# Attention layers of a twelve-layer stack: row maxima by half a batch, normalisation a batch ahead, one clamp a head, and another order of work in a head pair's step

## The chip, the cores and the metric

The kernel runs on one core of one Trainium2 chip and does the whole stack in one launch. The metric is device time in microseconds (us). Three runs of the kernel before took 2915.75, 2919.40 and 2923.68 us, with a median of 2919.4 us. The engines are TensorE (PE, with its weight loads as PEld), VectorE (DVE), ScalarE (ACT), GpSimd (POOL) and SyncE (SP), which issues most DMAs. Each engine takes its instructions in program order, and waits at the head of its queue until the semaphores that an instruction names have been counted up.

## The reference, cut to what matters

The input x is 8 batches of 256 tokens by 128 features. Twelve layers are added to it one after the other. Five of them are touched:

```python
def _L0_xattn_ref / _L3_xattn_ref(x, ctx, ...):      # 16 heads of 8, 512 context rows per batch
    q = x @ Wq + bq; k = ctx @ Wk + bk; v = ctx @ Wv + bv          # heads split after
    attn = softmax(q @ k.T * scale, axis=-1)                        # 256 x 512 per head
    out = (attn @ v) @ Wo + bo
def _L1_attn_ref(x, Wk, Wq, Wo, bo):                  # 16 heads of 8 over the 256 tokens, v = k
def _L2_attn_ref(x, Wq, Wkv, Wo, bo):                 # 16 heads of 64, causal, 256 x 256 per head
def _L3_attn_ref(x, w_down_q, w_down_kv, w_up_q, ...):# 16 heads of 64, low rank, rotary, not causal
    x = x + layer(layernorm(x))                       # for each; L2_attn: out / (sum + 1e-8)
```

In `L0_xattn` the probabilities are also held above a floor, exp(bounded max - clamp), that differs from row to row and head to head; this is the `clamp` branch of the kernel. The other seven layers (a gated recurrence, two single-head attentions, four feed-forward layers) are not touched.

## The kernel before

The layers run one after the other, each in its own block, with x (8 x 256 x 128) staying in SBUF. Within a layer every engine's program is a loop over steps n from FIRST to LAST, so the order on each engine is written out by hand. What one engine owes another is counted in semaphores. Two functions hold all five layers.

**16 heads of 8: `layer_attention_heads8` (L615 on), used by L0_xattn, L1_attn and L3_xattn.** One step is one head, so 128 steps carry the exponentials. Queries and keys are projected once per batch, split into three bf16 parts each (ACT L1123, L1125, then `split` at L813, L814, L816), written to DRAM in another order (`stage`, L754 and L760) and read back to all partitions (`spread`, L769 and L773). This preparation of a batch is the jobs T (transpose of the normalised rows), Q, K and V, all through the one PSUM bank `psM`. Each head is scored twice. The first time, LEAD steps ahead, PE L1045 puts queries on partitions and DVE L920 (L922 in L1_attn) takes the row maximum. When all 16 heads of a batch have their maxima, the job M turns them (PE L1027), they are negated and split into three bf16 parts (DVE L937 or ACT L1114, then POOL L851 to L857), and SP writes them as three more rows of the queries (`max_rows`, L780). The second time PE L1057 makes the turned scores with the maximum already subtracted, ACT L1160 takes the exponential, and PE L1071 (`weigh`) multiplies two heads with V. LEAD is H + 6 = 22 steps in the two layers with context and H + 10 = 26 in L1_attn; so 22 (26) steps pass with maxima alone before the first exponential, and as many at the end without maxima. In L0_xattn ACT makes the floor (L1146), SP writes it to DRAM and spreads all 16 heads' floors, 2 MB, over the partitions (L784, L787), and DVE L931 clamps each half head (128 x 512). In L3_xattn the result takes a way over DRAM (ACT L1140 out, SP L796 back, jobs A and O). `norm` on POOL normalises a batch at its own job T, and all copies of V are filled with ones by POOL (L866) before the first batch's splits. PE and DVE wait for all weights (`NLOAD`) before their first work.

**16 heads of 64: `layer_attention_heads64` (L174 on), used by L2_attn (causal) and L3_attn.** One step is one pair of heads, 64 steps in all, 8 in a batch. PE's step n: scores of pair n (L501), the jobs of slot n, `weigh` of pair n-2 (L536), the spread of 1/sum of pair n-2 over partitions (`spread_inverse`, L542), in the causal layer the blocking of later keys (L511), and the turning of pair n-1's probabilities (L521). Jobs are P (a later pair's projections, L468 or L475, in every step), V (values, L484, in steps 2 and 7 of a batch in L3_attn and in steps 0, 2, 3 and 7 in L2_attn), T and C (transpose, down-projection for the next batch), and O (output, L487, in steps 3 and 5); they share two PSUM banks `psA`. The product and the spread inverse lie in one bank, `psOR`. ACT copies the product out (`copy_out`, L601) after its exponentials (L588), and DVE multiplies that copy with the spread inverse (`combine`, L415) as the first thing of the next step, before it copies the turned probabilities (L400, causal) and takes the maxima (L392). In L3_attn DVE reads P into `rotc` and `rots` (L380), POOL adds them to `qk` (`rotate`, L306) and then widens the inverse (`widen`, L311).

## Time and profile before

The profiled execution took 2914.34 us, and the span of its trace is 2912.6 us. The five layers that are touched take 1876 us of it:

| layer | from, us | to, us | length, us | PE busy, us | DVE busy, us | POOL busy, us | granted TensorE clock |
|---|---|---|---|---|---|---|---|
| L0_xattn | 138.7 | 571.9 | 433.2 | 336.7 | 363.1 | 97.4 | 0.87 |
| L1_attn | 902.4 | 1123.9 | 221.5 | 186.2 | 116.1 | 62.5 | 0.85 |
| L2_attn | 1390.1 | 1784.2 | 394.1 | 346.8 | 219.5 | 52.3 | 0.98 |
| L3_attn | 2011.7 | 2447.9 | 436.2 | 356.3 | 239.9 | 149.2 | 0.93 |
| L3_xattn | 2448.8 | 2840.2 | 391.4 | 330.7 | 195.5 | 73.0 | 0.86 |

A layer begins when the one before has ended, so a layer's length is the sum of its steps, and what one step gains or loses comes back as often as it is repeated. Busy time of PE includes the pipeline's depth and is an upper bound of its work. The clock is a share of 2.4 GHz, and TensorE has two levels, 1.2 and 2.4 GHz: 0.87 means that it ran at the lower one for a part of the stretch.

### The profile page before, as it was taken

The numbers are of one execution on the slowest core, as the hardware profiler recorded it, in microseconds if no ns is written. First come the engines' busy times: TensorE is split into PE (matmuls) and PEld (weight loads), VectorE is DVE, ScalarE is ACT, GpSimd is POOL, SyncE is SP. The second block draws the span as 40 slices with busy tenths as digits, with TensorE's granted clock in tenths as the row PEclk, the third lists the DMA queues.
The fourth block names the chain that finished last, engine by engine and source line by source line (L and its number), as shares of the span: only waits on it lengthen the run. The fifth ranks groups of instructions, "written<-read, shape, count | busy, mean of one in ns | idle before, by whom it ended". The sixth has DMA issues, their size and how long they took to land. (4 is left out here: it accounts for less than half of the span.)

```text
span 2912.6 us, 40706 instructions
## 1 busy us (share of the span) xinstructions
PE 2224.6 (76%) x13779; PEld 1382.4 (47%) x13779; DVE 1690.1 (58%) x3810; ACT 1174.3 (40%) x2898; POOL 522.7 (18%) x703
## 2 busy tenths in 40 slices
PE   4668888789996897534799994936888886898982
PEld 2424343367774454423566663625555654344441
DVE  5568999633434562877456556562665554754524
ACT  3114444445552564211344441410555553354550
POOL 1122220000002410121111101011333322212100
PEclk9759999899997898866899997965999998698995
DMA  0043323110002310000000001011000001332200
GB/s 27 12 116 86 115 77 92 50 40 1 1 1 62 76 46 28 8 0 0 31 1 1 1 1 28 1 27 34 1 1 1 1 1 38 85 75 63 53 11 17
DMA packets 109272, 95.63 MB, mean 33 GB/s; under 512 B 61414, under 2 KB 96526, under 8 KB 105742
## 3 DMA queue, kind: packets, MB, share of 16 engines
q1 hardware_dynamic: 75790, 91.99, 12.2%
q10 hardware_dynamic: 33280, 1.05, 0.5%
q8 instruction: 113, 1.85, 0.3%
q14 instruction: 89, 0.73, 0.1%
HBM read 77.21 MB, written 14.81 MB: 32 GB/s over the span
## 5 line engine op out<-in xcount | busy, mean ns | idle before, releaser
L920 DVE TENSOR_REDUCE L_xattn_mx<-L_xattn_psS 128x1 f32<-128x512 f32 x512 | 326.9, 684 | 152.9 <-PE L_xattn_psS L1045 148.7
L1160 ACT ACTIVATE L_xattn_PT<-L_xattn_psT 128x512 f32<-128x512 f32 x512 | 284.7, 598 | 170.8 <-PE L_xattn_psT L1057 163.6
L1071 PE MATMUL L_xattn_psO<-L_xattn_PT,L_xattn_V 128*32 128x256 f32 x2048 | 264.1, 404 | 40.8 <-DVE L_xattn_PT L931 40.8
L588 ACT ACTIVATE L_attn_pr<-L_attn_psS,L_attn_negm 128x256 f32<-128x256 f32 (+1 forms) x512 | 222.4, 447 | 175.4 <-PE L_attn_psS L511 92.0
L1045 PE MATMUL L_xattn_psS<-L_xattn_KR,L_xattn_QR 72*128 72x512 bf16 x512 | 224.0, 441 | 56.3 <-DVE L_xattn_mx L920 30.0
L1057 PE MATMUL L_xattn_psT<-L_xattn_QR,L_xattn_KR 75*128 75x256 bf16 x1024 | 198.7, 283 | 3.0 <-ACT L_xattn_PT L1160 2.0
L1875 DVE TENSOR_TENSOR L_ffn_wt<-L_ffn_act,L_ffn_cw 128x512 f32<-128x512 f32 x128 | 88.5, 692 | 183.8 <-ACT L_ffn_act L1992 172.4
L1071 PEld LDWEIGHTS L_xattn_psO<-L_xattn_PT,L_xattn_V 128*32 128x32 f32 x2048 | 118.4, 115 | 154.6 <-issue 61.2
L931 DVE SCALAR_TENSOR_TENSOR L_xattn_PT<-L_xattn_PT,L_xattn_floor_w 128x512 f32<-128x512 f32 x256 | 178.4, 741 | 16.1 <-DMA L_xattn_floor_w<-L_xattn_staged_floor 11.6
L392 DVE TENSOR_REDUCE L_attn_mx<-L_attn_psS 128x2 f32<-128x512 f32 x256 | 164.4, 684 | 40.0 <-PE L_attn_psS L501 40.0
L415 DVE TENSOR_TENSOR L_attn_aoT<-L_attn_raw,L_attn_psOR 128x256 f32<-128x256 f32 x128 | 54.0, 422 | 222.7 <-ACT L_attn_raw L601 222.7
L501 PE MATMUL L_attn_psS<-L_attn_qk 64*128 64x256 f32 x1024 | 147.4, 405 | 30.0 <-ACT L_attn_pr L588 30.0
L1950 PE MATMUL L_ffn_psY<-L_ffn_wdn,L_ffn_fT 128*128 128x128 f32 x1024 | 138.4, 279 | 15.5 <-ACT L_ffn_fT L1997 8.6
L536 PE MATMUL L_attn_psOR<-L_attn_prT,L_attn_V 128*64 128x256 f32 (+1 forms) x1024 | 139.1, 382 | 7.3 <-DVE L_attn_prT L400 4.9
L1057 PEld LDWEIGHTS L_xattn_psT<-L_xattn_QR,L_xattn_KR 75*128 75x128 bf16 x1024 | 101.0, 102 | 80.1 <-issue 20.2
L1992 ACT ACTIVATE L_ffn_act<-L_ffn_psU 128x512 f32<-128x512 f32 x128 | 76.5, 597 | 145.6 <-PE L_ffn_psU L1925 145.6
L1045 PEld LDWEIGHTS L_xattn_psS<-L_xattn_KR,L_xattn_QR 72*128 72x128 bf16 x512 | 52.1, 102 | 173.2 <-DVE L_xattn_mx L920 111.8
L1950 PEld LDWEIGHTS L_ffn_psY<-L_ffn_wdn,L_ffn_fT 128*128 128x128 f32 x1024 | 125.1, 193 | 19.1 <-ACT L_ffn_fT L1997 10.3
L1925 PE MATMUL L_ffn_psU<-L_ffn_wup,L_ffn_hT 128*128 128x512 f32 x256 | 132.7, 602 | 0.0
L306 POOL TENSOR_TENSOR L_attn_qk<-L_attn_rotc,L_attn_rots 128x512 f32<-128x512 f32 x64 | 81.3, 1270 | 237.4 <-PE L_attn_psOR L542 130.3
L501 PEld LDWEIGHTS L_attn_psS<-L_attn_qk 64*128 64x128 f32 x1024 | 94.3, 188 | 58.5 <-issue 54.6
L521 PE MATMUL L_attn_psT<-ident,L_attn_pr 128*128 128x128 f32 x896 | 120.9, 276 | 0.0
(537 smaller groups left out, 4342.8 us busy)
## 6 DMA issues: line engine op xcount, KB each, us to landing
L_xattn_KR<-L_xattn_k_parts SPq DMA_DIRECT2D x96, 192.0 KB
L_xattn_floor_w<-L_xattn_staged_floor SPq DMA_DIRECT2D x8, 2048.0 KB, 8.2
L_xattn_QR<-L_xattn_q_parts SPq DMA_DIRECT2D x32, 288.0 KB
L_xattn_k_parts<-L_xattn_ks SPq DMA_DIRECT2D x48, 128.0 KB, 2.6
L_xattn_ctxT<-in_ctx SPq DMA_DIRECT2D x24, 192.0 KB, 2.4
L_attn_QR<-L_attn_q_parts SPq DMA_DIRECT2D x16, 288.0 KB
L_attn_KR<-L_attn_k_parts SPq DMA_DIRECT2D x48, 96.0 KB
L_xattn_q_parts<-L_xattn_qs SPq DMA_DIRECT2D x48, 64.0 KB, 2.5
```

Source lines behind the costliest of these rows:

```text
L392: link.mark(nc.vector.reduce_max(mx[:, n % 4, :, r], psS[g % 3][:], AX.X))
L501: ins = nc.tensor.matmul(psS[g % 3][:, t], qk[b % 2][at, j, 0, t * P:(t + 1) * P], qk[b % 2][at, j, 1], start=(t == 0 or not causal), stop ...
L536: ins = nc.tensor.matmul(psOR[r * DH:(r + 1) * DH, 0, first:S], V[b % 2][:, k, hd * DH:(hd + 1) * DH], prT[n % 2][:, r, k * S:k * S + widt ...
L588: ins = nc.scalar.activation(pr[n % 3][:, r, t, 0:width], psS[(2 * n + r) % 3][:, t, 0:width], ACT.Exp, bias=negm[:, n % 4, t, r:r + 1], s ...
L920: nc.vector.reduce_max(mx[:, b % 2, u, hd:hd + 1], psS[n % 2][:], AX.X).then_inc(s_used, 1)
L931: nc.vector.scalar_tensor_tensor(at, at, 1.0, floor_w[b % 2][:, hd, None, :].to_broadcast((P, 2, S)), ALU.min, ALU.max).then_inc(clamped, 1)
L1045: ins = nc.tensor.matmul(psS[n % 2][:, i * keys:(i + 1) * keys], QR[b % NB][0:PAIR, hd, t * P:(t + 1) * P], KR[b % NB][0:PAIR, hd, :], sta ...
L1057: ins = nc.tensor.matmul(psT[n % NPS][:, k], KR[b % NB][0:ROWS, hd, kt * P:(kt + 1) * P], QR[b % NB][0:ROWS, hd, :], start=True, stop=True)
L1071: ins = nc.tensor.matmul(psO[r:r + HW, g % 2], V[b % NV][:, kt, n % H], PT[(n * NU + kt // 2) % NPT][:, kt % 2], start=(kt == 0), stop=(kt ...
L1160: nc.scalar.activation(PT[i % NPT][:], psT[i % NPS][:], ACT.Exp).then_inc(exp_ready, 1)
L1925: nc.tensor.matmul(psU[n % 2][:], hT[b % 2][:, t * P:(t + 1) * P], wup[:, g * EG:(g + 1) * EG].rearrange("p e f -> p (e f)"), start=True, ...
L1950: ins = nc.tensor.matmul(psY[tile % 2][:, 0:D], fT[n % 3][:, k], wdn[:, g * BK + k], start=False, stop=(g == NGR - 1 and k == BK - 1))
```

## The change

**16 heads of 64.** A slot's jobs are parted into `early` (P) and `late` (all others; before step 0 all are early). PE's step is now: scores of n, spread inverse of n-2, early jobs, `weigh` of n-2, the blocking, late jobs, turning of n-1. ACT copies the spread inverse instead of the product (`copy_spread`), ahead of its jobs and exponentials; `weigh` waits for that copy, and `spread_inverse` waits for the `combine` of the pair before. DVE multiplies the product, read from PSUM, with the copy, for pair n-2 in step n, behind maxima, early jobs and the inverse.

**16 heads of 8.** LEAD falls by 8 steps, to HH + 6 = 14 and HH + 10 = 18 (HH = 8). The job M, the split of the maxima, their rows and the floors go by halves of a batch, 16 of each instead of 8. PREP goes from 42 to 38 and from 60 to 52 steps ahead. With context a batch is prepared in the order K, T, Q, and its K and Q DMAs change places. The floor's spread is 1 MB. A clamp takes a whole head (128 x 1024), and the probability tiles hold a head. Loads are waited for in three groups (`qk_loaded`, `v_loaded`, `o_loaded`), keys' and queries' first. POOL fills the first V ahead of the second `norm`, the others behind the first batch's splits, and normalises batch b+1 at the job Q of batch b.

```diff
@@ layer_attention_heads64
+    for n in range(0, LAST):
+        slots[n].sort(key=lambda group: group[0][0] != "P")
+    early = {n: [group for group in slots[n] if n < 0 or group[0][0] == "P"] for n in slots}
+    late = {n: [group for group in slots[n] if n >= 0 and group[0][0] != "P"] for n in slots}
...
             def combine(n):
                 b, j = n // NP, n % NP
-                dve.wait_ge(raw_ready, n + 1)
-                dve.wait_ge(r_ready, n + 1)
+                dve.wait_ge(pv_done, n + 1)
                 if j == 0 and b >= 2:
                     await_job(dve, ("O", b - 2, TB - 1))
-                nc.vector.tensor_tensor(aoT[b % 2][:, j], raw[n % 2][:], psOR[:, 1], ALU.mult).then_inc(ao_ready, 1)
+                nc.vector.tensor_tensor(aoT[b % 2][:, j], psOR[:, 0], spread[n % 2][:], ALU.mult).then_inc(ao_ready, 1)
...
             for n in range(FIRST, LAST):
-                if 0 <= n - 3 < NN:
-                    combine(n - 3)
                 if causal and 0 <= n - 2 < NN:
                     copy_turned(n - 2)
                 if 0 <= n < NN:
                     maxima(n)
-                for group in slots[n]:
+                for group in early[n]:
                     for job in group:
                         read(job)
                 if 0 <= n - 1 < NN:
                     invert(n - 1)
+                if 0 <= n - 2 < NN:
+                    combine(n - 2)
+                for group in late[n]:
+                    for job in group:
+                        read(job)
...
-                wait(pe, ao_ready, n)
+                pe.wait_ge(spread_ready, n + 1)
...
             def spread_inverse(n):
                 pe.wait_ge(rinv_ready, n + 1)
+                wait(pe, ao_ready, n)
...
                 if 0 <= n < NN:
                     scores(n)
-                for group in slots[n]:
+                if 0 <= n - 2 < NN:
+                    spread_inverse(n - 2)
+                for group in early[n]:
                     run(group)
                 if 0 <= n - 2 < NN:
                     weigh(n - 2)
-                    spread_inverse(n - 2)
                 if causal and 0 <= n < NN:
                     block_later(n)
+                for group in late[n]:
+                    run(group)
...
-            def copy_out(n):
+            def copy_spread(n):
                 act.wait_ge(r_ready, n + 1)
                 wait(act, ao_ready, n - 1)
-                nc.scalar.copy(raw[n % 2][:], psOR[:, 0]).then_inc(raw_ready, 1)
+                nc.scalar.copy(spread[n % 2][:], psOR[:, 1]).then_inc(spread_ready, 1)
@@ layer_attention_heads8
-    NPS, NPT = 3, 10 if NU == 2 else 8
+    NPS, NPT = 3, 5 if NU == 2 else 8
-    LEAD, PREP, STAGE, DVE_SPLITS = (H + 6, 42, 3, 2) if from_ctx else (H + 10, 60, 6, 3)
+    LEAD, PREP, STAGE, DVE_SPLITS = (HH + 6, 38, 3, 2) if from_ctx else (HH + 10, 52, 6, 3)
...
-        for i, kind in enumerate("TQK"):
+        for i, kind in enumerate("KTQ" if from_ctx else "TQK"):
             jobs[at + i * (b > 0)].append((kind, b, 0))
...
-        jobs[H * b - LEAD + H + 1].append(("M", b, 0))
+        for i in range(2):
+            jobs[H * b + HH * i - LEAD + HH + 1].append(("M", b, i))
...
-        stage_at = at + 2 + STAGE if b else FIRST
+        stage_at = min(at + 2 + STAGE, prep_step(b + 1) + 1) if b else FIRST
...
-        moves[H * b - LEAD + H + 1].append(("rows", b, 0))
+        for i in range(2):
+            moves[H * b + HH * i - LEAD + HH + 1].append(("rows", b, i))
...
                 for i in range(PARTS):
-                    sp.dma_start(QR[b % NB][PAIR + i:PAIR + i + 1], mp[:, i]).then_inc(m_rows, 16)
+                    sp.dma_start(QR[b % NB][PAIR + i:PAIR + i + 1, hf * HH:(hf + 1) * HH], mp[:, i]).then_inc(m_rows[hf], 16)
                 if clamp:
...
-                    wait(sp, clamped, NU * H * (b - 1))
-                    sp.dma_start(floor_w[b % 2][:].rearrange("p h s -> p (h s)"),
-                                 rows(f_dram.rearrange("h s -> (h s)")).to_broadcast((P, H * S))).then_inc(floor_spread, 16)
+                    wait(sp, clamped, HH * (n - 1))
+                    sp.dma_start(floor_w[n % 2][:].rearrange("p h s -> p (h s)"),
+                                 rows(f_dram.rearrange("h s -> (h s)")).to_broadcast((P, HH * S))).then_inc(floor_spread, 16)
...
             norm(0)
+            nc.gpsimd.memset(V[0][:], 1.0).then_inc(v_set, 1)
             norm(1)
-            for i in range(NV):
+            pool.wait_ge(k_split, SPLITS)
+            pool.wait_ge(q_split, SPLITS)
+            for i in range(1, NV):
                 nc.gpsimd.memset(V[i][:], 1.0).then_inc(v_set, 1)
...
-                    if kind == "T" and b >= 2:
-                        norm(b)
...
+                    if kind == "Q" and 1 <= b < B - 1:
+                        norm(b + 1)
...
-                nc.vector.scalar_tensor_tensor(at, at, 1.0, floor_w[b % 2][:, hd, None, :].to_broadcast((P, 2, S)), ALU.min, ALU.max).then_inc(clamped, 1)
+                nc.vector.scalar_tensor_tensor(at, at, 1.0, floor_w[half % 2][:, n % HH, None, :].to_broadcast((P, NKT, S)), ALU.min, ALU.max).then_inc(clamped, 1)
...
-            pe.wait_ge(loaded, 16 * NLOAD)
...
+                if b == 0 and kind in "QK":
+                    pe.wait_ge(qk_loaded, 16 * WQK)
```

The order of PE in one step of L3_attn with a value job, before: scores, P (wq, wk), values, `weigh`, spread inverse, turning.

```order
L501 MATMUL L_attn_psS<-L_attn_qk 128x256 x4
L475 MATMUL L_attn_psA<-L_attn_cT,L_attn_wq 128x256 x2
L475 MATMUL L_attn_psA<-L_attn_cT,L_attn_wk 128x256 x2
L484 MATMUL L_attn_psA<-L_attn_wv,L_attn_cT 128x512 x2
L536 MATMUL L_attn_psOR<-L_attn_prT,L_attn_V 64x256 x4
L542 MATMUL L_attn_psOR<-ident,L_attn_rinv 128x128 x2
L521 MATMUL L_attn_psT<-ident,L_attn_pr 128x128 x8
```

The same step on PE in the changed kernel, whose line numbers are a few higher (L507 scores, L549 spread inverse, L481 P, L542 `weigh`, L490 values, L527 turning):

```order
L507 MATMUL L_attn_psS<-L_attn_qk 128x256 x4
L549 MATMUL L_attn_psOR<-ident,L_attn_rinv 128x128 x2
L481 MATMUL L_attn_psA<-L_attn_cT,L_attn_wq 128x256 x2
L481 MATMUL L_attn_psA<-L_attn_cT,L_attn_wk 128x256 x2
L542 MATMUL L_attn_psOR<-L_attn_prT,L_attn_V 64x256 x4
L490 MATMUL L_attn_psA<-L_attn_wv,L_attn_cT 128x512 x2
L527 MATMUL L_attn_psT<-ident,L_attn_pr 128x128 x8
```

The spread inverse has moved from behind `weigh` to right behind the scores, and the values from ahead of `weigh` to behind it.

PE in L2_attn, before, in the step that has an output and a value job (L487, L484), up to the scores of the next step:

```order
L501 MATMUL L_attn_psS<-L_attn_qk 128x256 x4
L487 MATMUL L_attn_psA<-L_attn_wo,L_attn_aoT 128x128 x8
L468 MATMUL L_attn_psA<-L_attn_hT,L_attn_wq 128x256
L468 MATMUL L_attn_psA<-L_attn_hT,L_attn_wk 128x256
L484 MATMUL L_attn_psA<-L_attn_wv,L_attn_hT 128x512
L536 MATMUL L_attn_psOR<-L_attn_prT,L_attn_V 64x256 x2
L536 MATMUL L_attn_psOR<-L_attn_prT,L_attn_V 64x128 x2
L542 MATMUL L_attn_psOR<-ident,L_attn_rinv 128x128 x2
L511 MATMUL L_attn_psS<-L_attn_maskb,identb 128x128 x4
L521 MATMUL L_attn_psT<-ident,L_attn_pr 128x128 x6
```

The same step in the changed kernel:

```order
L507 MATMUL L_attn_psS<-L_attn_qk 128x256 x4
L549 MATMUL L_attn_psOR<-ident,L_attn_rinv 128x128 x2
L474 MATMUL L_attn_psA<-L_attn_hT,L_attn_wq 128x256
L474 MATMUL L_attn_psA<-L_attn_hT,L_attn_wk 128x256
L542 MATMUL L_attn_psOR<-L_attn_prT,L_attn_V 64x256 x2
L542 MATMUL L_attn_psOR<-L_attn_prT,L_attn_V 64x128 x2
L517 MATMUL L_attn_psS<-L_attn_maskb,identb 128x128 x4
L493 MATMUL L_attn_psA<-L_attn_wo,L_attn_aoT 128x128 x8
L490 MATMUL L_attn_psA<-L_attn_wv,L_attn_hT 128x512
L527 MATMUL L_attn_psT<-ident,L_attn_pr 128x128 x6
```

The blocking of later keys (maskb), for which the exponentials wait, now stands ahead of the output and value jobs instead of behind them.

PE ahead of the first turned scores of L0_xattn, before (L1045 scores for maxima, two a head; L1018 K, L1030 T, L1016 Q, L1021 V, L1027 the job M of all 16 heads, L1057 the first turned scores):

```order
L1018 MATMUL L_xattn_psM<-L_xattn_ctxT,L_xattn_wk 128x512
L1045 MATMUL L_xattn_psS<-L_xattn_KR,L_xattn_QR 128x512 x18
L1030 MATMUL L_xattn_psM<-ident,L_xattn_h 128x128 x2
L1045 MATMUL L_xattn_psS<-L_xattn_KR,L_xattn_QR 128x512 x2
L1016 MATMUL L_xattn_psM<-L_xattn_hT,L_xattn_wq 128x256
L1045 MATMUL L_xattn_psS<-L_xattn_KR,L_xattn_QR 128x512 x2
L1018 MATMUL L_xattn_psM<-L_xattn_ctxT,L_xattn_wk 128x512
L1045 MATMUL L_xattn_psS<-L_xattn_KR,L_xattn_QR 128x512 x4
L1021 MATMUL L_xattn_psM<-L_xattn_wv,L_xattn_ctxT 128x128 x4
L1045 MATMUL L_xattn_psS<-L_xattn_KR,L_xattn_QR 128x512 x2
L1027 MATMUL L_xattn_psM<-ident,L_xattn_mx 16x128 x2
L1045 MATMUL L_xattn_psS<-L_xattn_KR,L_xattn_QR 128x512 x11
```

The same stretch in the changed kernel (L1092 scores, L1068 V, L1065 K, L1077 T, L1063 Q, L1074 the job M of 8 heads, L1104 the first turned scores):

```order
L1063 MATMUL L_xattn_psM<-L_xattn_hT,L_xattn_wq 128x256
L1092 MATMUL L_xattn_psS<-L_xattn_KR,L_xattn_QR 128x512 x10
L1068 MATMUL L_xattn_psM<-L_xattn_wv,L_xattn_ctxT 128x128 x4
L1065 MATMUL L_xattn_psM<-L_xattn_ctxT,L_xattn_wk 128x512
L1092 MATMUL L_xattn_psS<-L_xattn_KR,L_xattn_QR 128x512 x2
L1077 MATMUL L_xattn_psM<-ident,L_xattn_h 128x128 x2
L1074 MATMUL L_xattn_psM<-ident,L_xattn_mx 8x128 x2
L1092 MATMUL L_xattn_psS<-L_xattn_KR,L_xattn_QR 128x512 x2
L1063 MATMUL L_xattn_psM<-L_xattn_hT,L_xattn_wq 128x256
L1092 MATMUL L_xattn_psS<-L_xattn_KR,L_xattn_QR 128x512 x9
L1104 MATMUL L_xattn_psT<-L_xattn_QR,L_xattn_KR 128x256 x2
```

M now follows 8 heads' scores instead of 16, and V stands next to K, T next to M, which before stood steps apart.

## Rows read from the trace of the kernel before

**Rows 1.** Windows of four layers: us, each engine's busy time, PE clock, DMA share, GB/s.
```profile
138.70:571.90 433.20, 336.69 (x2032) 159.92 (x2032) 363.14 (x637) 180.61 (x345) 97.38 (x122) 0.87 0.31 89
...
1390.10:1784.20 394.10, 346.76 (x2384) 241.38 (x2384) 219.51 (x592) 168.26 (x649) 52.29 (x108) 0.98 0.02 7
2011.70:2447.90 436.20, 356.34 (x2544) 245.04 (x2544) 239.85 (x560) 215.98 (x720) 149.15 (x201) 0.93 0.03 7
2448.80:2840.20 391.40, 330.71 (x2032) 156.55 (x2032) 195.51 (x381) 179.62 (x360) 73.04 (x105) 0.86 0.28 60
```

**Rows 2.** Windows of L3_attn: a plain step, a V step, an O+C step, a batch.
```profile
2192.21:2196.40 4.19, 4.19 (x36) 3.03 (x35) 3.08 (x7) 3.18 (x13) 1.62 (x3) 1.00 0.00 0
2196.40:2205.40 9.00, 6.93 (x39) 4.38 (x38) 4.79 (x10) 4.58 (x17) 3.15 (x4) 0.81 0.01 2
2218.38:2227.23 8.85, 7.54 (x55) 5.55 (x54) 3.90 (x8) 3.63 (x13) 4.49 (x6) 1.00 0.01 2
2240.40:2291.17 50.77, 43.36 (x319) 29.90 (x318) 29.96 (x71) 26.92 (x91) 18.58 (x25) 0.97 0.00 1
```

**Rows 3.** Timeline of L3_attn: start us, us, engine, line, what, idle time before.
```profile
2200.43 0.33 PEld L484 LDWEIGHTS L_attn_psA<-L_attn_wv,L_attn_cT 64*128 64x128 f32 x4 [2.44 <-DVE L_attn_rotc L380]
...
2208.99 0.70 PE L475 MATMUL L_attn_psA<-L_attn_cT,L_attn_wq 64*128 64x256 f32 x4 [0.47 <-DVE x L374]
...
2210.13 0.69 DVE L380 TENSOR_TENSOR L_attn_rotc<-L_attn_psA,L_attn_cosT 128x512 f32<-128x512 f32 x1 [1.28 <-PE L_attn_psA L475]
...
2211.55 1.27 POOL L306 TENSOR_TENSOR L_attn_qk<-L_attn_rotc,L_attn_rots 128x512 f32<-128x512 f32 x1 [8.12 <-PE L_attn_psOR L542]
...
2212.77 0.39 POOL L311 COPY L_attn_rinv<-L_attn_inv 128x256 f32<-128x256 f32 x1
```

**Rows 4.** Timeline of L2_attn, one turn of the loop in a step without other jobs.
```profile
1500.15 0.42 DVE L415 TENSOR_TENSOR L_attn_aoT<-L_attn_raw,L_attn_psOR 128x256 f32<-128x256 f32 x1 [1.52 <-ACT L_attn_raw L601]
...
1502.96 0.40 PE L511 MATMUL L_attn_psS<-L_attn_maskb,identb 128*128 128x128 bf16 x4 [0.17 <-DVE L_attn_negm L394]
...
1504.42 1.13 PE L501 MATMUL L_attn_psS<-L_attn_qk 64*128 64x256 f32 x8 [0.41 <-ACT L_attn_pr L588]
...
1505.38 0.42 DVE L415 TENSOR_TENSOR L_attn_aoT<-L_attn_raw,L_attn_psOR 128x256 f32<-128x256 f32 x1 [2.19 <-ACT L_attn_raw L601]
```

**Rows 5.** Window of one batch of L2_attn.
```profile
1493.69:1539.89 46.20, 42.48 (x298) 29.57 (x299) 27.40 (x74) 20.81 (x82) 6.44 (x13) 1.00 0.00 1
```

**Rows 6.** Windows of L0_xattn: maxima alone, both, no maxima.
```profile
165.50:205.90 40.40, 34.12 (x68) 9.76 (x69) 33.31 (x63) 6.75 (x12) 13.37 (x20) 0.50 0.34 86
214.80:521.00 306.20, 250.13 (x1624) 123.75 (x1626) 283.21 (x493) 141.58 (x268) 67.04 (x81) 0.94 0.32 90
521.00:571.90 50.90, 41.56 (x314) 20.92 (x308) 33.98 (x60) 26.22 (x54) 4.49 (x5) 0.93 0.11 43
```

**Rows 7.** ACT L1160 alone in windows of L1_attn (two), then L3_xattn (three).
```profile
1068.20:1086.60 18.40, 9.23 (x16) 1.00 0.01 2
1103.40:1118.00 14.60, 8.49 (x15) 1.00 0.01 1
2735.60:2770.80 35.20, 17.96 (x32) 1.00 0.28 56
2598.70:2643.50 44.80, 17.97 (x32) 0.92 0.28 63
2803.80:2828.30 24.50, 14.99 (x30) 1.00 0.09 9
```

**Rows 8.** DVE lines of 214.8 to 521.0 us: count, busy us, mean ns, idle.
```profile
L931 DVE SCALAR_TENSOR_TENSOR L_xattn_PT<-L_xattn_PT,L_xattn_floor_w 128x512 f32<-128x512 f32 x209 | 147.8, 748 | 5.4 <-DMA L_xattn_floor_w<-L_xattn_staged_floor 5.4
```

**Rows 9.** Timeline: an operation of 1024 columns; a cast in L0_xattn's start.
```profile
107.45 1.22 DVE L1537 SCALAR_TENSOR_TENSOR L_attn_hm<-L_attn_psA,L_attn_h 128x1024 f32<-128x1024 f32 x1 [0.88 <-PE L_attn_psA L1606]
...
149.89 3.92 DVE L814 CAST L_xattn_qs<-L_xattn_qf 128x256 bf16<-128x256 f32 x1
```

**Rows 10.** DMA issues of the page: count, KB each, median us to landing.
```profile
L_xattn_floor_w<-L_xattn_staged_floor SPq DMA_DIRECT2D x8, 2048.0 KB, 8.2
```

198 lines of the change are left out of this document (113 added, 85 removed).

## The prediction

> **What bounds the kernel now.** I first read the windows of the layers [rows 1]. TensorE is busy 82% of L3_attn and 88% of L2_attn, VectorE 84% of L0_xattn, and nothing is above 90%: each layer has waits that its loop repeats. So I cut each layer into steps at the first matmul of a step. In L3_attn a step with no job beside P takes 4.19 us with TensorE busy throughout; that is its bound. Steps with a value job (9.00 us, clock 0.81) or output and C (8.85) are far longer than their work, and a batch of eight takes 50.77 [rows 2]. L2_attn takes 46.20 a batch [rows 5]; its timeline shows a closed ring, one turn 5.23 us: combine, copy, maxima, blocking, exponentials, copy-out, combine, in which TensorE idles 0.41 + 0.17 [rows 4]. In L0_xattn I cut where the maxima run alone, where maxima and clamps run together (VectorE busy 283 of 306 us) and where no maxima are left [rows 6].
>
> **L3_attn (436.2 us).** Nothing is added or removed: one ACT copy takes the place of another of 128 x 256. The order decides. Before, a V job waits 2.44 us until VectorE has read the P banks that it reuses [rows 3]; behind that idle time the clock is at its lower level (1.2 GHz) for a part of the step. Now `weigh` (about 1.0 us) and the spread inverse (0.3) stand ahead of V, so the wait shrinks to about 0.8 and, I take it, the clock stays up. VectorE's part up to the read is unchanged: V can start 4.1 us into the step, takes 0.9, the turning 1.0: 6.0 us instead of 9.00. The highest it can be is 7.4, what V steps take before in the batches where the clock held. T, O and C get the same cover: they reuse P's banks too.
>
> Against this, the spread inverse now stands right behind the scores and waits for POOL, whose `widen` is queued behind `rotate`. That is a new ring: P to rotc 1.14, rotc to rotate 1.42, rotate to widen 1.22 (start to start), widen 0.39 [rows 3], spread about 0.27: 4.44 us. It holds a plain step at up to 4.4 instead of 4.19. Queued behind the waiting spread on TensorE are P, `weigh` and all else.
>
> A batch, slots 0 to 7, by this: 4.2, 4.4, 6.0, 6.3, 4.7, 6.7, 4.2, 6.1 = 42.6 against 50.8. That is 8.2 in a middle batch, 9.8 in two where both V steps slow down, less in the last (no jobs for a next one): -60 us. Bounds: 0 (all waits only move) and -83 (64 steps at 4.19 plus the jobs' own 6 us a batch and 36 us of start and end, from 436.2).
>
> **L2_attn (394.1).** Combine and copy-out leave the ring. What stays: scores, spread, P, `weigh`, blocking, the exponentials of one head, next scores. Before, blocking to next scores took 1.46 and scores to blocking 5.23 - 1.46 = 3.77, of which 0.17 was idle and some is the next job's [rows 4]: together 4.9. TensorE alone needs 5.23 - 0.58 = 4.65. So three plain steps save 0.3 each, three V steps (V now runs under the exponentials) 0.4, the V+O step 0.5, the O step 0.1, a batch 2.7 of 46.20 [rows 5]: -20 us. Bounds 0 and 8 x 0.58 x 8 = -37.
>
> **Shorter lead (L0_xattn, L1_attn, L3_xattn).** Eight steps of maxima alone at the start and eight without maxima at the end become eight full steps. In L0_xattn the first kind costs 40.4 / 22 = 1.84, but two batches' preparations stay in it; its floor is two maxima of some 0.69. I take 1.45, nearer the floor: -11.6. The second kind: 24.5 / 15 = 1.63 [rows 7]: -13.1. A full step: 306.2 / 104 = 2.94 [rows 6]: +23.5.
> - L0_xattn besides: the first clamp waits from 205.9 to 214.8 for the floors. Small DMAs of this kind take under 2 us, so of the 8.2 [rows 10] I let 1.7 be fixed and halve the rest: -3.2, and as much less the second time at the end (-1.7, part covered). One clamp of 1024 columns for two of 512: 2 x 0.69 (what L380 takes for 512 columns [rows 3]; the clamps' own mean is 0.748 [rows 8]) - 1.22 [rows 9] = 0.16 a head, on the bound: -18 over 113 heads; ends 0 and 2 x 0.748 - 1.22 = 0.28 a head. Eight more bounded maxima +3. K and V in one step, T and M in the next: +5. A half's chain (M, split, rows, floor out, floor back) took 18.5 us for 16 heads, so 15 for 8, with five steps of 2.85 to cover it, and POOL now has K's split just ahead: +5. Sum with the start's -5: -16.
> - L3_xattn: full step 35.2 / 16 = 2.2 [rows 7], so -11 - 13.1 + 17.6 = -6.5. A batch that prepares another takes 44.8 against 35.2; half of that is the output job's transpose waiting for the read-back, which is queued on SP behind `stage`. The new table puts `stage` three steps later, but one more M chain ahead of each read-back. I take 2.5 of the 9.6 in five batches, -12.5, and +2 for the other M. With the start -5: -22.
> - L1_attn: full 18.4 / 16 = 1.15, end 14.6 / 15 = 0.97 [rows 7], start 0.75 (one maximum, 0.69, is the floor): -4.6; M jobs +2.5; start -5.3: -7.5.
> - The starts: a cast of 128 x 256 takes 3.92 us while POOL fills V [rows 9], 0.42 being what an operation of this size needs [rows 4]: -3.5; the rest from not waiting for all eight loads. Each between 0 and -8.
>
> **Sum.** -60 - 20 - 16 - 7.5 - 22 = -125.5 us. The profiled execution took 2914.34, so 2789; it ran 5.1 us below the median of the runs shown, 2919.4. The forecast for the median is 2794 us, 4.3% less.
>
> **A rule that speaks against it.** An operation of 512 columns takes 0.69 us undisturbed, the clamps' mean is 0.748 [rows 3, 8], and the 3.92 us cast ran beside POOL's fills [rows 9]: the two engines hold each other up. The Trainium skill (SBUF — State Buffer, Who interferes with whom) says that a VectorE instruction with two SBUF inputs takes an exclusive lock against a GpSimd one that reads SBUF, held for the whole instruction. The trace agrees in kind. By that rule the clamp of 1024 columns holds POOL off nearly twice as long a time; its result is the second rival.
>
> **Rivals.**
> - The ring through POOL in L3_attn is longer than its parts: spans on POOL are rough, TensorE idles over 1 us in every step and falls to the lower clock, as in the V steps. For it: 0.81 in [rows 2]. Against it: plain steps now show POOL with 1.62 of 4.19 busy. Price 64 x 1 us: 2858. It decides above 0.5 us a step.
> - POOL waits behind the longer clamps in L0_xattn: up to 1.22 - 0.75 = 0.5 us for each of the 5 to 8 operations of a half's chain, which already fills its window: 42 us over 14 halves: 2836.
> - The shorter lead gives nothing: preparations and DMA chains, not maxima, set the starts (DMA share 0.34, clock 0.50 in the first window [rows 6]), and the full steps cost what the ends give back: 43 us less gain: 2837.
> - Slower: every half's chain misses its window in both layers with context. Nothing covers it and VectorE stands, as it stood 8.9 us at the first clamp. 15 halves x 8.9 in L0_xattn and 16 x 1 in L3_xattn: +150, 2944. It decides from 4.2 us a half on, over 30 halves. Against it: between its first and last batch L0_xattn waited for floors 5.4 us in all [rows 8].
>
> **How the numbers follow.** Forecast 0.66; ring through POOL 0.10; clamps and POOL 0.09; lead without gain 0.12; slower 0.03. Two rivals at once are within 2880. The bounds of the unknown terms (V steps 6.0 to 7.4, starts, M windows) give the forecast 2755 to 2835 by itself; with two of three rivals 2750 to 2850. A measurement of this kernel tells 0.3% (9 us) from no change; faster 0.95, same 0.02, slower 0.03.
>
> **What would show it.** L3_attn near 376 us with V steps near 6.0 and clock 1.00; wrong if they stay above 7.4. TensorE's spread inverse there waits for POOL L315, 0.1 to 0.3 a step. L2_attn near 374, its plain step 4.9, with the scores still waiting for an exponential and VectorE's multiply no longer waiting for ACT. L0_xattn near 417, L1_attn 214, L3_xattn 369; the clamp at 1.22 us; the first exponentials 16 us sooner in their layer; waits for floor_w under 15 us in all. If L0_xattn keeps its length, the halves' chains are at fault; if L3_attn does, the ring.

## The result, and the profile after

The changed kernel took 2788.4 us (median of 4 runs, 2785.0 to 2795.1); the kernel before took 2917.7 beside it. The ratio is 0.9556, with a 95% interval of 0.9532 to 0.9580. The forecast was 2794 us. The profiled execution has a span of 2788.4 us, against 2912.6 before. The sum was right; several of its terms were not, as the windows of the five changed layers show, in the program's order (L0_xattn, L1_attn, L2_attn, L3_attn, L3_xattn), columns as in [rows 1]:

```profile
139.44:566.29 426.85, 335.69 (x2048) 162.39 (x2048) 347.54 (x517) 184.54 (x353) 136.50 (x162) 0.87 0.33 90
897.06:1111.17 214.11, 183.79 (x1248) 101.31 (x1248) 112.20 (x226) 112.27 (x241) 75.61 (x126) 0.87 0.24 63
1374.69:1726.90 352.21, 326.98 (x2384) 229.17 (x2384) 233.58 (x592) 174.64 (x649) 52.07 (x108) 0.98 0.02 7
1950.62:2339.74 389.12, 354.09 (x2544) 232.71 (x2544) 233.79 (x560) 219.95 (x720) 148.04 (x201) 0.96 0.03 8
2339.74:2717.37 377.63, 324.33 (x2048) 157.70 (x2048) 191.14 (x381) 182.59 (x376) 86.71 (x129) 0.87 0.29 63
```

These windows run from a layer's first instruction to the next layer's. Cut in the same way, the layers of before took 434.2, 222.5, 395.0, 437.1 and 392.4 us, so the differences are:

| layer | forecast | measured |
|---|---|---|
| L0_xattn | -16 | -7.3 |
| L1_attn | -7.5 | -8.4 |
| L2_attn | -20 | -42.7 |
| L3_attn | -60 | -48.0 |
| L3_xattn | -22 | -14.8 |
| five layers | -125.5 | -121.2 |

The other layers gave 3 more, all of it in L2_ffn, which took 112.4 to 118.6 us in kernels that have the same code there: nothing of the change.

How much does one profile of a layer say? The changed L0_xattn was profiled in five kernels that leave its code alone: 426.9, 430.6, 420.0, 421.6 and 426.9 us, mean 425.2. L3_xattn in the same five: 375.2 to 380.1, mean 377.8. L1_attn 211.2 to 214.3, mean 212.9. The 16x64 layers repeat within 2.2 us (L3_attn 388.6 to 390.8 in seven kernels with the same code). L0_xattn of before took 434.2 and, where only the 16x64 layers differ, 430.7: by means the change is -7.2 there. Below, 16x8 layers are held against these means, and less than 5 us in L0_xattn is read as nothing.

**L2_attn.** One turn of the loop in a step without other jobs. First more rows of TensorE's turn before, from the same batch as [rows 4] (start, duration, engine, line, what, idle time before):

```profile
1499.19 1.14 PE L501 MATMUL L_attn_psS<-L_attn_qk 64*128 64x256 f32 x8 [0.40 <-ACT L_attn_pr L588]
1500.25 0.70 PE L468 MATMUL L_attn_psA<-L_attn_hT,L_attn_wq 128*128 128x256 f32 x2
1500.49 1.02 DVE L400 COPY L_attn_prT<-L_attn_psT 128x384 f32<-128x384 f32 x2
...
1501.31 1.11 PE L536 MATMUL L_attn_psOR<-L_attn_prT,L_attn_V 128*64 128x256 f32 x8
1502.35 0.44 PE L542 MATMUL L_attn_psOR<-ident,L_attn_rinv 128*128 128x128 f32 x2
```

And the turn of the changed kernel:

```profile
1474.16 1.13 PE L507 MATMUL L_attn_psS<-L_attn_qk 64*128 64x256 f32 x8
1474.21 1.01 DVE L404 COPY L_attn_prT<-L_attn_psT 128x384 f32<-128x384 f32 x2
1475.22 0.44 PE L549 MATMUL L_attn_psOR<-ident,L_attn_rinv 128*128 128x128 f32 x2
1475.50 0.60 PE L474 MATMUL L_attn_psA<-L_attn_hT,L_attn_wq 128*128 128x256 f32 x2
...
1476.45 0.87 PE L542 MATMUL L_attn_psOR<-L_attn_prT,L_attn_V 128*64 128x256 f32 x8
...
1477.26 0.40 PE L517 MATMUL L_attn_psS<-L_attn_maskb,identb 128*128 128x128 bf16 x4
...
1477.37 0.42 DVE L418 TENSOR_TENSOR L_attn_aoT<-L_attn_psOR,L_attn_spread 128x256 f32<-128x256 f32 x1 [0.20 <-PE L_attn_psOR L542]
...
1478.72 1.13 PE L507 MATMUL L_attn_psS<-L_attn_qk 64*128 64x256 f32 x8 [0.40 <-ACT L_attn_pr L598]
```

The multiply (L418) is now behind the copies of the turned probabilities (L404) and waits for weigh alone. The turn takes 4.56 us, not 5.23 and not the forecast 4.9. Blocking to the next scores is 1.46 us as before [rows 4], with the same 0.40 of idle time. All of the gain is between scores and blocking: 3.77 us before, 3.10 now.

**L3_attn.** Windows of the changed kernel: a plain step, a V step and a middle batch, as [rows 2]:

```profile
2113.34:2118.01 4.67, 4.61 (x36) 2.92 (x35) 3.14 (x7) 3.40 (x14) 1.66 (x3) 1.00 0.00 0
2118.01:2124.21 6.20, 5.73 (x40) 3.25 (x39) 4.05 (x9) 3.65 (x14) 2.70 (x4) 1.00 0.01 3
2108.80:2153.30 44.50, 43.46 (x319) 28.62 (x318) 29.05 (x71) 27.50 (x91) 18.46 (x25) 1.00 0.01 1
```

A V step fell from 9.00 us (7.39 where the clock had held) to 6.20 and holds the full clock. But a plain step rose from 4.19 to 4.54 or 4.67, in which TensorE is still busy nearly throughout.

### The profile page after: what moved, and what is told of

The parts are those of the page before. It is cut to its first block and busy times, and to the rows that moved or that the text cites. A ratio compares the mean times of both kernels' runs of the same rounds, so it can differ in the third digit from the quotient of the medians.

```text
span 2788.4 us, 41069 instructions
## 1 busy us (share of the span) xinstructions
PE 2195.0 (79%) x13827; PEld 1363.7 (49%) x13827; DVE 1674.2 (60%) x3690; ACT 1196.5 (43%) x2938; POOL 587.1 (21%) x791
## 5 line engine op out<-in xcount | busy, mean ns | idle before, releaser
L1092 PE MATMUL L_xattn_psS<-L_xattn_KR,L_xattn_QR 72*128 72x512 bf16 x512 | 216.5, 427 | 46.1 <-DVE L_xattn_mx L964 22.6
L396 DVE TENSOR_REDUCE L_attn_mx<-L_attn_psS 128x2 f32<-128x512 f32 x256 | 165.0, 686 | 114.7 <-PE L_attn_psS L507 114.6
L1104 PE MATMUL L_xattn_psT<-L_xattn_QR,L_xattn_KR 75*128 75x256 bf16 x1024 | 201.1, 283 | 2.8 <-ACT L_xattn_PT L1208 1.4
L1118 PEld LDWEIGHTS L_xattn_psO<-L_xattn_PT,L_xattn_V 128*32 128x32 f32 x2048 | 118.6, 116 | 149.7 <-issue 58.7
L975 DVE SCALAR_TENSOR_TENSOR L_xattn_PT<-L_xattn_PT,L_xattn_floor_w 128x1024 f32<-128x1024 f32 x128 | 162.7, 1275 | 11.8 <-DMA L_xattn_floor_w<-L_xattn_staged_floor 6.0
L507 PE MATMUL L_attn_psS<-L_attn_qk 64*128 64x256 f32 x1024 | 146.0, 403 | 11.9 <-ACT L_attn_pr L598 11.9
L1104 PEld LDWEIGHTS L_xattn_psT<-L_xattn_QR,L_xattn_KR 75*128 75x128 bf16 x1024 | 102.5, 102 | 79.5 <-issue 17.8
L542 PE MATMUL L_attn_psOR<-L_attn_prT,L_attn_V 128*64 128x256 f32 (+1 forms) x1024 | 125.3, 365 | 6.5 <-ACT L_attn_spread L611 6.5
L966 DVE TENSOR_REDUCE L_attn_mx<-L_attn_psS 128x2 f32<-128x512 f32 x128 | 86.8, 690 | 64.4 <-PE L_attn_psS L1092 62.6
L1092 PEld LDWEIGHTS L_xattn_psS<-L_xattn_KR,L_xattn_QR 72*128 72x128 bf16 x512 | 52.3, 102 | 147.8 <-DVE L_xattn_mx L964 86.9
L527 PE MATMUL L_attn_psT<-ident,L_attn_pr 128*128 128x128 f32 x896 | 121.2, 275 | 0.0
L527 PEld LDWEIGHTS L_attn_psT<-ident,L_attn_pr 128*128 128x128 f32 x896 | 100.3, 141 | 38.4 <-issue 26.7
```

The source lines that it names most:

```text
L396: link.mark(nc.vector.reduce_max(mx[:, n % 4, :, r], psS[g % 3][:], AX.X))
L507: ins = nc.tensor.matmul(psS[g % 3][:, t], qk[b % 2][at, j, 0, t * P:(t + 1) * P], qk[b % 2][at, j, 1], start=(t == 0 or not causal), stop ...
L527: ins = nc.tensor.transpose(psT[r][:, at:at + P], pr[n % 3][:, r, t, k * P:(k + 1) * P], m.ident[:])
L975: nc.vector.scalar_tensor_tensor(at, at, 1.0, floor_w[half % 2][:, n % HH, None, :].to_broadcast((P, NKT, S)), ALU.min, ALU.max).then_inc( ...
L1092: ins = nc.tensor.matmul(psS[n % 2][:, i * keys:(i + 1) * keys], QR[b % NB][0:PAIR, hd, t * P:(t + 1) * P], KR[b % NB][0:PAIR, hd, :], sta ...
L1104: ins = nc.tensor.matmul(psT[n % NPS][:, k], KR[b % NB][0:ROWS, hd, kt * P:(kt + 1) * P], QR[b % NB][0:ROWS, hd, :], start=True, stop=True)
```

## The experiments

Each kernel is the changed one with the edit shown, unless said otherwise. The times of single profiles below are spans of layers.

**The two halves of the 16x64 change.** First the jobs go back beside P, behind it in the same place (before the change an output job stood ahead of P):

```diff
-    early = {n: [group for group in slots[n] if n < 0 or group[0][0] == "P"] for n in slots}
-    late = {n: [group for group in slots[n] if n >= 0 and group[0][0] != "P"] for n in slots}
+    early = {n: [group for group in slots[n] if True] for n in slots}
+    late = {n: [group for group in slots[n] if False] for n in slots}
```

> The changed kernel, with all jobs of a step (V, T, C, O) back beside P, ahead of weigh and blocking; the spread inverse stays early and is copied. Theory (cover): in L3_attn the gain comes from the jobs standing behind weigh, so that VectorE's reads of the P banks have time to end. V steps go back from 6.2 to 7.4 or more, C and O steps rise too, a batch from 44.5 to 49 or 50: L3_attn 389 to about 427. In L2_attn the gain comes from combine and copy-out leaving the ring, so its plain step stays at 4.57 and the layer within 6 us of 352. Rival (the early spread made both gains): L3_attn stays within 6 us of 389.

The second kernel is the one before with the late jobs alone: `for group in slots[n]` is split into `early[n]` at its old place and `late[n]` behind `spread_inverse`, blocking, `invert` and `exps`.

> The kernel before, with only the jobs other than P moved behind weigh, spread inverse and blocking; the spread inverse stays behind weigh and is multiplied out of its bank. Theory: L3_attn has the cover and not the ring through POOL, so its plain step is 4.19 and not 4.54, its V steps 6.1: a batch about 43, L3_attn about 378, that is 11 less than in the changed kernel. L2_attn keeps its ring and its plain step of 5.23: within 6 us of 394. Rival (the cover needs the spread inverse ahead of P): L3_attn stays above 410.

Windows of L2_attn and L3_attn, first of the kernel with the jobs beside P, then of the one with late jobs alone:

```profile
1372.37:1743.78 371.41, 330.00 (x2384) 234.57 (x2384) 230.99 (x592) 174.66 (x649) 52.08 (x108) 0.98 0.02 7
1967.45:2396.90 429.45, 359.00 (x2544) 232.29 (x2544) 236.40 (x560) 219.25 (x720) 150.09 (x201) 0.96 0.03 7
```

```profile
1386.06:1766.24 380.18, 349.00 (x2384) 237.16 (x2384) 222.46 (x592) 168.32 (x649) 52.08 (x108) 0.98 0.02 7
1988.65:2366.08 377.43, 339.50 (x2544) 239.40 (x2544) 234.21 (x560) 214.08 (x720) 147.82 (x201) 0.96 0.03 8
```

In L3_attn the late jobs alone give -59.7 us; the early spread inverse alone gives -7.7, and added to the late jobs it costs 11.7. So the whole gain of this layer is the cover, and the other half of the change takes a fifth of it back. In L2_attn the early spread alone gives -23.6, the late jobs alone -14.8, both -42.7. Here I missed: I had expected the late jobs to give L2_attn under 6 us. A batch of 46.2 falls to 44.6, and the gain is not in the steps that hold V or O: two of these are shorter and three longer, 0.1 us in all. It is in the three others, each of which follows a step with a late job: 4.65, 4.66 and 4.80 us instead of 5.23. The loop of before was no rigid ring.

**Why a plain step of L3_attn rose.** Two kernels take POOL out of the way. In one the spread inverse stands behind P:

```diff
-                if 0 <= n - 2 < NN:
+                if causal and 0 <= n - 2 < NN:
                     spread_inverse(n - 2)
                 for group in early[n]:
                     run(group)
+                if not causal and 0 <= n - 2 < NN:
+                    spread_inverse(n - 2)
```

> The changed kernel, in L3_attn the spread inverse right behind P and no longer right behind the scores. Theory (POOL ring): P is no longer queued behind the wait for widen, so P to rotc to rotate to widen is no ring over a step; the plain step falls from 4.54 to 4.2 or 4.3, V steps stay at 6.2: a batch from 44.5 to about 42.5, L3_attn from 389 to about 374. Rival (plain steps are held by the copy of the spread inverse on ScalarE, which weigh waits for): the copy now comes 1 us later and the step grows to 4.7 or more: L3_attn 392 or above.

In the other, in L3_attn, VectorE's `invert(n - 1)` moves ahead of `early[n]` and POOL's `widen(n - 1)` ahead of `rotate`:

> The changed kernel, in L3_attn VectorE inverts the sums ahead of its reads of P, and POOL widens ahead of rotate. Theory (POOL ring): widen no longer waits for rotate, the spread inverse no longer for widen; plain step from 4.54 to 4.2: L3_attn from 389 to about 374. Rival (the step is held by something else on TensorE or ScalarE): 389, within 3 us. Other rival (qk comes late because rotate is now second): scores wait for POOL, L3_attn above 392.

Both theories failed, and in both runs a stated rival came true: L3_attn took 402.5 us with the spread behind P and 387.6 with widen first. With widen first the one plain step of 4.67 in a batch falls to 4.53 and the others stay. So the ring through POOL is worth 1.5 us at most. TensorE's plain step with widen first, from its timeline:

```profile
2112.67 1.14 PE L509 MATMUL L_attn_psS<-L_attn_qk 64*128 64x256 f32 x8
2113.73 0.44 PE L551 MATMUL L_attn_psOR<-ident,L_attn_rinv 128*128 128x128 f32 x2
2114.10 0.70 PE L483 MATMUL L_attn_psA<-L_attn_cT,L_attn_wq 64*128 64x256 f32 x4
...
2115.16 1.08 PE L544 MATMUL L_attn_psOR<-L_attn_prT,L_attn_V 128*64 128x256 f32 x8
2116.18 1.09 PE L529 MATMUL L_attn_psT<-ident,L_attn_pr 128*128 128x128 f32 x8
2117.20 0.49 PE L509 MATMUL L_attn_psS<-L_attn_qk 64*128 64x256 f32 x2
```

There is no idle time in any row, and still the step takes 4.53. The same engine in the kernel with late jobs alone:

```profile
2103.17 1.14 PE L508 MATMUL L_attn_psS<-L_attn_qk 64*128 64x256 f32 x8
2104.14 0.60 PE L482 MATMUL L_attn_psA<-L_attn_cT,L_attn_wq 64*128 64x256 f32 x4
...
2105.10 1.08 PE L543 MATMUL L_attn_psOR<-L_attn_prT,L_attn_V 128*64 128x256 f32 x8
2106.12 0.44 PE L549 MATMUL L_attn_psOR<-ident,L_attn_rinv 128*128 128x128 f32 x2
2106.39 1.04 PE L528 MATMUL L_attn_psT<-ident,L_attn_pr 128*128 128x128 f32 x8
2107.36 0.49 PE L508 MATMUL L_attn_psS<-L_attn_qk 64*128 64x256 f32 x2
```

Start to start, with the spread between scores and P: 1.06 (scores), 0.37 (spread), 1.06 (P), 1.02 (weigh), 1.02 (turning). With the spread between weigh and turning: 0.97 (scores), 0.96 (P), 1.02 (weigh), 0.27 (spread), 0.97 (turning). The same 34 matmuls cost 0.34 us more where the 128-row transposes stand between two kinds of matmul that work on 64 rows; beside the turning, which is the same kind, they add their own 0.27 us and nothing more. These losses are called breaks below. The rows show where they fall; what in the engine makes them, no run here shows. A batch of the changed kernel takes 44.5 us against 43.0: three plain steps pay 0.35 to 0.5 us each, the five with jobs under 0.1. Eight batches make the 11.7 us.

With the spread behind P another thing happens:

```profile
2110.23 0.44 PE L549 MATMUL L_attn_psOR<-ident,L_attn_rinv 128*128 128x128 f32 x2
2111.13 1.08 PE L542 MATMUL L_attn_psOR<-L_attn_prT,L_attn_V 128*64 128x256 f32 x8 [0.46 <-ACT L_attn_spread L613]
```

Weigh waits 0.46 us for ScalarE's copy, the rival of that run's expectation: the step is 4.87. A further kernel tested the breaks by putting the spread inverse where they should cost nothing, behind the turning of the step before (it also has widen first in L3_attn):

```diff
                 if 0 <= n - 1 < NN:
                     turn_probs(n - 1)
+                    spread_inverse(n - 1)
```

> The changed kernel with the spread inverse of a group at the end of the step before, right behind the turning of probabilities (the same kind of transposes), in both 16x64 layers; in L3_attn VectorE inverts and POOL widens first. Theory (breaks): in L3_attn the spread inverse between scores and P costs TensorE 0.35 us a step where the kinds of matmuls change, and behind the turning it costs its own two transposes only; the plain step falls from 4.53 to 4.2, L3_attn from 389 to 370 or 375. In L2_attn it leaves the stretch between scores and blocking, 0.27 us, and fills the idle time of 0.40 ahead of the scores: plain step 4.57 to 4.3, L2_attn from 352 to 337. Rival (the breaks are no cost of their own, ScalarE or VectorE set 4.53): L3_attn stays at 388. Rival for L2_attn (blocking waits for VectorE's maxima anyway): 352.

L3_attn took 404.0 us, 29 to 34 more than expected, and L2_attn 350.8, 14 more. The timeline of its L3_attn says why:

```profile
2114.16 1.14 PE L509 MATMUL L_attn_psS<-L_attn_qk 64*128 64x256 f32 x8
2115.13 0.60 PE L483 MATMUL L_attn_psA<-L_attn_cT,L_attn_wq 64*128 64x256 f32 x4
...
2116.09 1.08 PE L544 MATMUL L_attn_psOR<-L_attn_prT,L_attn_V 128*64 128x256 f32 x8
...
2118.67 0.41 PE L551 MATMUL L_attn_psOR<-ident,L_attn_rinv 128*128 128x128 f32 x2 [0.47 <-DVE L_attn_aoT L418]
```

Scores and P are back at 0.97 and 0.96 us, so the breaks went as expected. But the spread inverse now waits for the multiply that reads its bank, which on VectorE stands behind both reads of P: a wait took the place of the breaks, and a larger one. In L2_attn the plain step fell from 4.57 to 4.39 us, with 4.3 expected, while V and O steps rose by 0.04; why it gained no more, no run here shows.

**The clamp.** Back to two operations of 512 columns:

```diff
-                nc.vector.scalar_tensor_tensor(at, at, 1.0, floor_w[half % 2][:, n % HH, None, :].to_broadcast((P, NKT, S)), ALU.min, ALU.max).then_inc(clamped, 1)
+                for u in range(2):
+                    at = PT[n % NPT][:, 2 * u:2 * u + 2]
+                    ins = nc.vector.scalar_tensor_tensor(at, at, 1.0, floor_w[half % 2][:, n % HH, None, :].to_broadcast((P, 2, S)), ALU.min, ALU.max)
+                ins.then_inc(clamped, 1)
```

> The changed kernel with the clamp of a head as two operations of 512 columns again (L0_xattn only). My prediction priced the single clamp at 2 x 0.69 - 1.22 = 0.16 us a head, 18 us. New reading: two clamps run one into the other, start to start 1.20 us for the pair and 1.28 to the second's end, against 1.22 for the one: 0.07 us a head. By that L0_xattn rises from 427 by 9 us or less; by the prediction's price it rises by 18. Where VectorE does not bound the step at all: 0, within 2 us.

L0_xattn took 441.1 us, 16 over its mean and 10.5 over the highest of its five profiles. That is near the prediction's 18 and more than the 9 of my second reading, though with one profile, and a spread of 5 us to either side, it is no exact price. The price was about right for a reason that it didn't have. Left alone, a pair of clamps takes 1.28 us from the first's start to the second's end, and the one clamp 1.22: over 128 heads 8 us. But summed over the layer, from first start to last end, the pairs take 181.2 us here and 179.3 in the kernel before, the single clamps 163.2. Beyond their undisturbed length that is 17 us for the pairs and 7 for the single clamps. The long ones are those that run beside POOL: of 128 pairs 20 took 1.7 us or more, of the single clamps 7, and all of these overlap an operation of POOL. POOL pays for it in part. Its cast of negm in the layer's middle, with two clamps a head and then with one:

```profile
L894 POOL CAST L_xattn_mp<-L_xattn_negm 8x256 bf16<-8x256 f32 x14 | 5.4, 388 | 2.4 <-POOL L_xattn_negm L890 2.4
```

```profile
L894 POOL CAST L_xattn_mp<-L_xattn_negm 8x256 bf16<-8x256 f32 x15 | 9.8, 652 | 2.6 <-POOL L_xattn_negm L890 2.6
```

This is the second rival's mechanism, seen at 0.26 us an operation. Not every operation pays: another cast of the same chain (L897) took 0.45 us beside the single clamps and 0.64 beside the pairs. Over the layer POOL was busy 136.5 us with the single clamps and 124.8 with the pairs. But a half's chain from the bounded maxima to the issue of the floors took 8.2 us before and 8.3 to 9.3 in all but two halves now, and nothing came of it.

**The lead.** The first kernel takes the long leads back, with the maxima still by halves:

```diff
-    LEAD, PREP, STAGE, DVE_SPLITS = (HH + 6, 38, 3, 2) if from_ctx else (HH + 10, 52, 6, 3)
+    LEAD, PREP, STAGE, DVE_SPLITS = (H + 6, 46, 3, 2) if from_ctx else (H + 10, 60, 6, 3)
```

> The changed kernel with the leads of before (22 and 26 steps, preparations 46 and 60 steps ahead) and the maxima's chain still by halves, so eight steps before a half's exponentials more. If the shorter lead made the gains: L0_xattn +1 to +5 (start and end cost 15 more and full steps give 23 back, as the prediction's terms 11.6 + 13.1 - 23.5 have it: nearly nothing), L1_attn +5, L3_xattn +7. If it did not: all three within 2 us. First exponential of L0_xattn about 8 steps of maxima alone later, +9 us.

L0_xattn fell by 10 us to 414.9, L1_attn rose by 4, L3_xattn fell by 4. This edit moved something else too: the preparations went to other slots, and K no longer shares a step with V. So it had to be held against a kernel with the short lead in which V stands alone (`LATE_V = 11` for `H + 6`):

> The changed kernel with the value job of a batch in the layers with context in a step of its own (slot 5 of a batch) and no longer in K's step. Theory (jobs that share the one bank psM in one step make each other wait): the two long steps of K and V and of M and T (in L0_xattn together 10.4 to 11.4 us for four heads' steps worth 9.3, in L3_xattn 5.6 + 4.0 with 3.4 of idle TensorE) lose the wait for VectorE's read of V, 1.1 us a batch: L0_xattn -5 to -8, L3_xattn -5 to -8. Rival (a step with V costs the same wherever it is): both within 2 us.

L0_xattn 416.5 (-8.7) and L3_xattn 370.2 (-7.5), where -5 to -8 was expected for each. Between these two kernels the long lead is worth -1.7 in L0_xattn and +3.1 in L3_xattn. The next pair is cleaner, though not clean: in it, too, the preparations lie in other slots of a batch (12 to 14 and 4 to 6), and V (5 and 10). First the short lead, with the preparations moved as well, so that no step but one (A and Q in L3_xattn, in both kernels of the pair) holds two jobs on the bank psM:

```diff
-    LEAD, PREP, STAGE, DVE_SPLITS = (HH + 6, 38, 3, 2) if from_ctx else (HH + 10, 52, 6, 3)
-    LATE_V = H + 6
+    LEAD, PREP, STAGE, DVE_SPLITS = (HH + 6, 36, 3, 2) if from_ctx else (HH + 10, 52, 6, 3)
+    LATE_V = 11
```

> The kernel with the value job in slot 5 of a batch, and besides the preparations two steps later (K in slot 12, T 13, Q 14; M stays in 3 and 11), so that no step holds two jobs but A and Q in L3_xattn. If jobs on the one bank psM wait for each other only when they share a step, M and T no longer do: M waits 6.7 us in all for ScalarE's read of T in both layers. L0_xattn -4 against the kernel with the value job alone moved (416.5), L3_xattn -4 against its 370.2. Rival (the preparation's chain over POOL and the DMAs then comes too late for its half): L0_xattn or L3_xattn rises by 5 or more.

and then the long lead, spread in the same way (`H + 6, 44` and `H + 10, 60`, LATE_V as it was):

> The changed kernel with the long leads (22 and 26 steps) and the chain still by halves, preparations at 44 and 60 steps: K in slot 4, T 5, Q 6, V 10, M 3 and 11, so no two jobs in a step, as in the run with the jobs spread. That run and this one differ in the lead alone. By my prediction's terms the short lead is worth 11.6 + 13.1 - 23.5 = 1 us in L0_xattn, 7 in L3_xattn and 5 in L1_attn: L0_xattn 409, L3_xattn 356, L1_attn 219. Rival (lead gives nothing): L0_xattn and L3_xattn within 3 of 407.5 and 349.4. Other rival (the longer lead covers the chain, so the clock holds): L0_xattn 400 or less.

Windows of L0_xattn, L1_attn and L3_xattn, short lead and long lead:

```profile
139.72:547.18 407.46, 327.00 (x2048) 161.73 (x2048) 345.26 (x517) 184.21 (x353) 136.10 (x162) 0.88 0.34 94
878.04:1092.16 214.12, 183.84 (x1248) 101.25 (x1248) 112.17 (x226) 112.28 (x241) 75.68 (x126) 0.87 0.25 63
...
2325.50:2674.94 349.44, 306.81 (x2048) 153.89 (x2048) 191.53 (x381) 181.20 (x376) 86.65 (x129) 0.91 0.31 68
```

```profile
140.62:547.82 407.20, 332.05 (x2048) 160.79 (x2048) 347.31 (x517) 183.46 (x353) 136.27 (x162) 0.88 0.33 94
878.82:1097.65 218.83, 187.01 (x1248) 100.62 (x1248) 111.64 (x226) 111.89 (x241) 76.11 (x126) 0.86 0.24 62
...
2330.42:2692.81 362.39, 318.95 (x2048) 153.75 (x2048) 190.89 (x381) 182.05 (x376) 87.15 (x129) 0.89 0.30 65
```

In this pair the short lead is worth nothing in L0_xattn, 5 us in L1_attn and 13 in L3_xattn. The cut says more. From the first scores to the first turned ones it saves 10.2 us in L0_xattn and 9.9 in L3_xattn, and 9.8 and 9.9 in the pair before. From there to the last turned scores L0_xattn loses 10.1 (11.8 in the pair before); L3_xattn gains 2.7 here and lost 6.7 there. So the saving at the start is firm, and what L3_xattn makes of it, 3 or 13 us, hangs on the slots of the jobs.

Spreading the jobs over steps is worth 18 us in L0_xattn and 28 in L3_xattn against the changed kernel. Against the kernel with V alone it is 9 and 21, where I had expected 4 and 4 from the idle times that I had counted. The timeline of TensorE in the changed L3_xattn shows the start of it, at the two steps that hold V and K, and T and M:

```profile
2503.68 1.10 PE L1065 MATMUL L_xattn_psM<-L_xattn_ctxT,L_xattn_wk 96*128 96x512 f32 x2 [1.07 <-DVE L_xattn_V L950]
2506.22 0.41 PE L1077 MATMUL L_xattn_psM<-ident,L_xattn_h 128*128 128x128 f32 x2 [0.57 <-ACT L_xattn_ks L1174]
2508.02 0.58 PE L1074 MATMUL L_xattn_psM<-ident,L_xattn_mx 128*8 128x128 f32 x2 [1.39 <-ACT L_xattn_hT L1155]
```

Each job waits until the one before has been read out of the bank they share: 3.03 us idle within 5.4. What follows is dearer. The windows of the half batch without preparations, of the one with them, and of the stretch from M's matmul on:

```profile
2480.70:2497.50 16.80, 16.54 (x122) 8.22 (x121) 10.69 (x19) 10.22 (x21) 1.71 (x3) 1.00 0.51 104
2497.50:2523.90 26.40, 23.12 (x137) 11.55 (x136) 12.35 (x27) 12.52 (x26) 9.50 (x14) 0.87 0.20 45
2508.30:2523.90 15.60, 15.47 (x91) 7.61 (x90) 7.05 (x13) 7.35 (x16) 7.64 (x12) 0.79 0.29 63
```

and the same two halves with the jobs spread (the one with preparations first):

```profile
2435.50:2455.50 20.00, 18.71 (x129) 9.44 (x128) 11.47 (x23) 12.46 (x26) 8.01 (x12) 1.00 0.18 38
2455.50:2472.70 17.20, 17.07 (x130) 9.27 (x129) 11.57 (x23) 10.12 (x21) 3.21 (x6) 1.00 0.58 125
```

Behind the three waits TensorE is busy 15.47 of 15.60 us, but its granted clock is 0.79: a part of the stretch ran at 1.2 GHz instead of 2.4. With the jobs spread the clock stays at 1.00 and this batch takes 37.2 us instead of 43.2. Five batches have such a half (23.0 to 26.4 us, 19.5 to 20.0 with the jobs spread), which is 25 of the 28 us. The fifth tells the waits from the clock: it has the same 3.0 us of idle time as the third, its clock stayed at 1.00, and it took 23.0 us. The third, whose windows are shown, took 26.4 with the clock at 0.87. The kernel with V alone lies between: 2.0 us idle in such a half, clock 0.86, 23.8 us; with all jobs spread 1.0 us idle, clock 1.00, 20.0 us. One microsecond less of waiting gave 3.8.

In L0_xattn the same halves fall from 25.4 to 28.5 us to 22.1 to 23.5, and their idle time on TensorE by 1.5 us; their clock was 0.87 to 1.00 and is 0.93 to 1.00. How the rest of its 18 us comes about, these runs do not show.

**POOL's fills.** All V buffers are filled ahead of the first splits again:

```diff
-            nc.gpsimd.memset(V[0][:], 1.0).then_inc(v_set, 1)
             norm(1)
-            pool.wait_ge(k_split, SPLITS)
-            pool.wait_ge(q_split, SPLITS)
-            for i in range(1, NV):
+            for i in range(NV):
```

> The changed kernel with POOL filling all V buffers with ones ahead of the first splits, as before. Prediction's price for this: 3.5 us a layer (a cast of 3.92 us for 0.42). Expected: first scores of L0_xattn from 22.9 to 26 us after the layer's start, of L1_attn and L3_xattn likewise by 3 us; the layers +3 each. If the loads and the DMA chain set the start: 0.

The first scores came 1.4 us later in L0_xattn, 4.0 in L1_attn and 2.9 in L3_xattn. L1_attn rose by 4.8 us to 217.7; L3_xattn (379.8) and L0_xattn (421.7) stayed inside the spread of their five profiles. So the price of about 3.5 is shown for L1_attn alone.

**The version that follows.** Spread jobs in the 16x8 layers; in L3_attn the spread inverse behind weigh and multiplied out of its bank, as before the change, with the late jobs kept; L2_attn as changed.

> The changed kernel with the jobs of the 16x8 layers spread as in the run before (value job in slot 5, preparations in 12 to 14), and in L3_attn the spread inverse behind weigh and multiplied out of its bank, as before the change, with the late jobs kept; L2_attn as changed. Theory (breaks): L3_attn 377.4 as with the late jobs alone, 11.7 less than now; the rest as in the run before. Sum 2748 - 11.5 = 2736 us, ratio to the kernel before 0.938. Rival (the two do not add up, since each sets the other's clock): 2748.

It took 2735.3 us (median of 4, 2730.8 to 2738.7), ratio to the kernel before 0.9376 (0.9351 to 0.9401). L3_attn took 377.8, L0_xattn 407.5, L3_xattn 351.3: the parts add up. That is 53 us less than the changed kernel, whose runs were made at another time, against the same kernel before.

## Why the prediction was right in sum and wrong in parts

That the sum came within 6 us of the median is in part luck. L2_attn gave 22.7 us more than its term and L1_attn 0.9; L3_attn gave 12.0 less, L0_xattn 8.7 and L3_xattn 7.2, and a layer that was not touched gave 3.

**Late jobs in L3_attn: right mechanism, and nearly the size.** V steps 6.20 us for a forecast 6.0, the clock at 1.00 where it had been 0.81. Alone they gave -59.7 us. The forecast's -60 was for the whole change of the layer, which gave -48.0: a batch was to take 42.6 and took 44.5, of which 0.9 is in the three plain steps, 0.5 in the step with O and C (7.23 for 6.7) and the rest in the others.

**The ring through POOL in L3_attn: wrong mechanism.** It was to hold a plain step at up to 4.4; the step is 4.54. But with widen ahead of rotate, so that no such ring exists, it is 4.53; only one plain step in a batch waits for POOL, 0.13 us. What stands in the ring's place are 0.34 us of breaks on TensorE itself, which I had not priced: I took the moved operation at its own duration, "nothing is added or removed". The first rival, a longer ring, falls with it.

**L2_attn: the gain mis-sized by half, and beyond my bound.** The term was 0.3 us a plain step, "together 4.9"; it measured 0.67. I counted 3.77 less 0.17 from scores to blocking as work that stays. 0.50 of it went too: weigh takes 0.81 start to start and not 1.04, since VectorE's copies of the turned probabilities, no longer behind the multiply, end ahead of it. The kernel with late jobs alone has both cases: 0.80 us where the copies end before `weigh` starts, 1.16 where they end 0.3 us after. And the spread inverse takes 0.28 where it and the idle time took 0.61, and P takes 0.95 instead of 1.06. The bound of -37 counted only the idle time of the trace; `weigh` at 1.04 had no idle time in its row and still held 0.23 us that could go.

**The clamp: right in size, by luck.** 0.13 us a head of VectorE's time against the kernel before, 0.14 against the run with two clamps, instead of 0.16; about 16 us of the layer for 18. I had subtracted a duration that overlaps its neighbour's (two in a row start 0.60 us apart, and each lasts 0.68), which alone would have given too much; the time beside POOL made it good.

**L0_xattn, cut at its marks.** First scores come 4.0 us sooner after the layer's start (forecast 5), the stretch to the first turned scores is 7.0 shorter (forecast 11.6), and from there to the last ones it is 3.3 longer in this pair of profiles, 3.9 by the means of five after (360.2) and two before (356.3), where the forecast has 0.5. In that last term stands the one that I mis-sized most, the next. The stretch to the first turned scores was over-priced: eight steps of maxima alone are worth 10.2 us and not 11.6, and that stretch is 33.4 us long with K and V, T and M in shared steps and 31.9 with the jobs spread.

**L3_xattn, cut likewise:** first scores 6.2 us sooner (forecast 5), the stretch to the first turned scores 6.8 shorter (forecast 11), and from there on 1.8 shorter (forecast 6).

**Two jobs in a step: wrong size, by far.** I priced K and V, T and M together at +5 in L0_xattn and at nothing in L3_xattn. They cost 18 and 28 against the same jobs spread, with the reservation that this run also moved them to other slots. The step of the argument that failed is that a wait costs its own length: in L3_xattn it also costs the clock behind it. Some of that was there before the change, at other slots [rows 7]: a prepared batch took 44.8 us then and 43.2 after.

**The shorter lead:** forecast -1 in L0_xattn, -6.5 in L3_xattn and -4.6 in L1_attn. Measured were 0, -13 and -5 with the jobs spread, and +2, -3 and -6 in the pair before. The third rival (no gain) holds for L0_xattn alone. The first exponentials came 11 us sooner in L0_xattn, 7 in L1_attn and 13 in L3_xattn; I had said 16.

**The waits for floors** were 6 us in all in the stretch with clamps, under the 15 forecast, so the slower rival never came near: a half's chain, from the bounded maxima to the issue of the floors, takes as long as that for a whole batch (8.3 to 9.3 us for 8.2, twice 11), but it is covered.

## What to carry to other kernels

When a job is moved, look at what stands on either side of it on its own engine, and at which bank or tile it shares with its new neighbours: here the neighbours were worth 18, 28 and 12 us, and the sum had 5, 0 and less than 2 for them. An idle time that recurs on TensorE is to be priced with the clock behind it, so read the granted clock of the stretch that follows. A sum that comes out right proves none of its terms: cut it by layer before you believe it.

## What the runs showed of the hardware

- On TensorE a pair of 128-row transposes between two groups of 64-row matmuls cost 0.34 us more than beside other transposes: from the last pair of scores to it 0.31 us instead of 0.21, from it to what follows 0.20 instead of 0.11, between the first two pairs of P 0.31 instead of 0.21, and 0.06 because a run of transposes now starts twice in a step. In L2_attn, where P works on 128 rows, P follows the two transposes after 0.11 us and only the way from the scores to them costs 0.31.
- Two VectorE operations of 512 columns took 1.28 us against 1.22 for one of 1024. Beside POOL the two are disturbed more than the one: 17 us against 7 over 128 heads, while POOL was busy 136.5 us in the layer beside the single clamps and 124.8 beside the pairs.
- In kernels whose L0_xattn is the same code, the layer took 420.0 to 430.6 us. The steps that differ take 3.58 us in one batch and about 5.0 in another. In one of the long ones, 16 matmuls of weigh took 3.31 us instead of 1.92 at a granted clock of 0.57, behind idle times of 1.06 and 0.52 us: the clock falls in some batches and not in others.
